# Role adapter with layer norm on one core: the b_up add on VectorE, role rows broadcast by DMA per batch, four raw slots for x and W_down

## The chip, the cores and the metric

The kernel runs on one core of one Trainium2 chip. Times are device microseconds (us) of one execution; the comparison figure is the median of several executions. Inside a core TensorE (PE) multiplies matrices, VectorE (DVE), ScalarE (ACT) and GpSimd (POOL) work on vectors, and SyncE (SP) here only issues DMAs. Each engine runs its own instruction list in order and waits on semaphores.

## The reference

Eight batches of 512 tokens of width 1024. Each batch b has a role r in {1, 2}, known only at run time, which picks one of three weight sets.

```python
# x: (8, 512, 1024); role: (8,)
h = einsum('bsh,bhk->bsk', x, W_down[role]) + b_down[role]     # 1024 -> 512
h = gelu(h)                                                    # exact form
u = einsum('bsk,bkh->bsh', h, W_up[role]) + b_up[role]         # 512 -> 1024
y = x + u
yn = (y - mean(y)) * rsqrt(var(y) + 1e-5)                      # over the 1024
return yn * gamma[role] + beta[role]
```

## The kernel before, in words

**The product.** Each float32 operand is split in two parts of the reduced float32 format that TensorE takes: `hi` is the rounded value (a cast by ScalarE), `lo` is the remainder (a subtraction by VectorE). A product is the sum of three passes, hi x hi, hi x lo, lo x hi. A batch has 96 "down" matmuls (x transposed and W_down, result `down_ps`, the hidden width in four groups `kc` of 128) and 96 "up" matmuls (h and W_up, result `up_ps`, four token tiles `t` of 128 tokens x 1024, two at a time in `up_ps`). The host gives x in both layouts, `xT` for the product and `x` for the residual sum.

**Staging.** x and W_down come in `NLOAD` = 4 parts of 512 KB each, W_up in 4 parts, the residual rows in 4 tiles, all 512 KB. The raw parts of x and W_down share `NSTAGE` = 2 slots each, so the load of part i waits for the split of part i - 2 (`x_split`, `wd_split`). W_up has one slot per part.

**The order within a batch** is written out by hand for each engine. TensorE (L284 to L332): down parts 0 and 1 over all four `kc`; then for each `kc` parts 2 and 3, so that the four groups end one after the other (`down_ready`); then up tile by tile, where tile 0 waits for `wu_split` and `h_split` of each `kc`, and each tile waits until the half of `up_ps` that it overwrites has been summed (`summed`). ScalarE (L395 to L421): casts of W_up, then for each `kc` gelu and the cast of h, between them the casts of the next batch's x and W_down parts, then for each tile the mean and the squares in two halves of 512. VectorE (L546 to L570): `wu_lo` (L551), then `h_lo` (L555) for each `kc` with `x_lo` (L480) and `wd_lo` (L485) of the next batch between them, then for each tile the sum with the row total (L497), the centring with gamma (L515) and the finish with rstd and beta (L526). The first two tiles have a next-batch split ahead of the sum. `h_full` is used again for the centred tiles, so gelu waits for `normed` of the batch before.

**GpSimd** (L444 to L461) adds b_up of the batch's role to the four tiles of residual rows (L449, `biased`, on which the sum waits), then computes rstd of each tile in three operations of 128x1. At the start it spreads b_up, gamma and beta of all three roles over the partitions (L468) from rows that SP loads into `rows`; every engine then picks the role's slice through a register. SP may not load `rows` of batch 0 before that (`params_spread`).

**SyncE** (L201 to L234) issues every DMA, in one queue: next batch's parts 0 and 1 of x and W_down, rows 0 and 1, next part 2, rows 2, next part 3, rows 3, next W_up, then the four stores as the tiles are finished. `load_rows` of a tile waits until the tile's last store has landed (`stored`).

The loop over batches 1 to 6 is a hardware loop; batch 0 and batch 7 are unrolled. In the last batch the last tile is summed in two halves.

Of the kernel before, what the change touches and what calls it, by code (L numbers as in the profile page):

```python
# [5 lines left out]
P = 128  # L23
LN_EPS = 1e-05

ALU = mybir.AluOpType
# [7 lines left out]
def bass_role_adapter_layernorm(  # L34
# [14 lines left out]
    HC = H // P  # L49
# [6 lines left out]
    NSTAGE = 2  # L56
    WARM_UP = 12
    assert KC == NLOAD and S == BANK and K == BANK and HALVES == 2 and NT == 4

    with ExitStack() as ctx:  # L60
# [17 lines left out]

# [6 lines left out]
        b_up_all = sb("b_up_all", [P, R * H], F32)  # L85
        gamma_all = sb("gamma_all", [P, R * H], F32)
        beta_all = sb("beta_all", [P, R * H], F32)
# [9 lines left out]
        var = sb("var", [P, NT, HALVES], F32)  # L97
        var_eps = sb("var_eps", [P, NT, 2], F32)
# [5 lines left out]

# [3 lines left out]

        roles_landed = sem("roles_landed")
        b_down_landed = sem("b_down_landed")  # L110
        params_landed = sem("params_landed")
        x_landed = [sem(f"x_landed{i}") for i in range(NSTAGE)]
        wd_landed = [sem(f"wd_landed{i}") for i in range(NSTAGE)]
        first_chunk_landed = sem("first_chunk_landed")
# [7 lines left out]
        first_chunk_hi = sem("first_chunk_hi")  # L122
# [20 lines left out]
        var_ready = sem("var_ready")  # L143
        half_var_eps_ready = sem("half_var_eps_ready")
        params_spread = sem("params_spread")
# [7 lines left out]
        def landed(batch, i):  # L153

            return 16 * ((NLOAD // NSTAGE) * batch + i // NSTAGE + 1)
# [5 lines left out]
        params = [(rows[32 * i:32 * i + 1, :, :].rearrange("p t h -> p (t h)")[:, 0:R * H], all_roles, param)  # L161
                  for i, (all_roles, param) in enumerate(((b_up_all, b_up), (gamma_all, gamma), (beta_all, beta)))]

        centred = h_full[:, :, :].rearrange("p (t i) s -> p t (i s)", t=2)

# [9 lines left out]

        @block.sync
        def _(sp):
            def load_x_part(batch, i):
                sp.dma_start(x_stage[:, i % NSTAGE, :],
                             xT[batch].rearrange("(p n c) s -> p n (c s)", n=NLOAD, c=CPL)[:, i, :]  # L180
                             ).then_inc(x_landed[i % NSTAGE], 16)

            def load_wd_part(role, i):
                sp.dma_start(wd_stage[:, i % NSTAGE, :],
                             W_down[role].rearrange("(p n c) k -> p n (c k)", n=NLOAD, c=CPL)[:, i, :]
                             ).then_inc(wd_landed[i % NSTAGE], 16)

            def load_first_wd_part(role):

                src = W_down[role].rearrange("(p c) k -> p (c k)", c=HC)  # L190
                sp.dma_start(wd_stage[:, 0, 0:K], src[:, 0:K]).then_inc(first_chunk_landed, 16)
                sp.dma_start(wd_stage[:, 0, K:CPL * K], src[:, K:CPL * K]).then_inc(wd_landed[0], 16)

            def load_wu_part(role, i):
                sp.dma_start(wu_stage[:, i, :],
                             W_up[role, i * P:(i + 1) * P, :]).then_inc(wu_landed[i], 16)

            def load_rows(batch, t):
                sp.dma_start(rows[:, t, :], x[batch, t * P:(t + 1) * P, :]).then_inc(rows_landed[t], 16)

            def steps(b):  # L201
                first, last = is_first(b), is_last(b)
                if not last:
                    next_role = load_role(sp, b + 1)
                    for i in range(NSTAGE):
                        sp.wait_ge(x_split, NLOAD * b + NLOAD - NSTAGE + i + 1)
                        load_x_part(b + 1, i)
                        sp.wait_ge(wd_split, NLOAD * b + NLOAD - NSTAGE + i + 1)
                        load_wd_part(next_role, i)
                if first:  # L210
                    sp.wait_ge(params_spread, len(params))
                for t in range(NT):
                    if not first:
                        sp.wait_ge(stored[t], 16 * b)
                    load_rows(b, t)
                    if not last and t in (1, 2):
                        i = NLOAD // 2 + t - 1
                        sp.wait_ge(x_split, NLOAD * (b + 1) + i - NSTAGE + 1)
                        load_x_part(b + 1, i)
                        sp.wait_ge(wd_split, NLOAD * (b + 1) + i - NSTAGE + 1)  # L220
                        load_wd_part(next_role, i)
# [4 lines left out]
                for t in range(NT):  # L226
                    if is_last(b) and t == NT - 1:
                        for i in range(HALVES):
                            sp.wait_ge(normed, NT * B + i)
# [27 lines left out]
            for t in range(NT - 1):  # L257
                sp.wait_ge(stored[t], 16 * B)
# [354 lines left out]
```

## Time and profile before

| what | value |
|---|---|
| three executions | 407.95, 413.99, 415.98 us; median 413.99 |
| the profiled execution's span | 407.0 us (the lowest of the three times is 0.95 above it) |
| busy: PE / DVE / ACT / POOL | 369.9 / 312.0 / 193.2 / 163.5 us |
| matmuls | 1548, 12 of them a warm-up |
| DMA | 84.05 MB, mean 206 GB/s |
| mean granted TensorE clock | 0.954 |

The profile gives one execution. A busy time is the union of an engine's instructions; matmuls overlap in the pipeline, so their step (start to start) says more than their duration. The granted clock is a share of full speed, 2.4 GHz; 0.5 is 1.2 GHz.

### The profile page before, as it was taken

To read this page: it belongs to the slowest core of one execution; us is meant where nothing else is said; L and a number is where in the kernel's file an instruction comes from. 1 tells how busy PE (TensorE), PEld (TensorE's weight loads), DVE (VectorE), ACT (ScalarE), POOL (GpSimd) and SP (SyncE) were. 2 spreads that over 40 slices of the span, in tenths; PEclk is the share of its full clock that TensorE was granted. 3 is DMA by queue.
4 is the path that set the end of the run, shared out by engine and by line. 5 is a ranking of instruction groups with operands and counts; after the bars stand their busy time and mean duration, and the time that the engine had idled before them with its cause. 6 is when DMAs were issued, how large, how long until landed. Compare 5 with 4: busy or idle time off the path is not lost.

```text
span 407.0 us, 5068 instructions
## 1 busy us (share of the span) xinstructions
PE 369.9 (91%) x1548; PEld 298.2 (73%) x1548; DVE 312.0 (77%) x262; ACT 193.2 (47%) x358; POOL 163.5 (40%) x138
## 2 busy tenths in 40 slices
PE   6969879988999799997999979997999959999992
PEld 2748668866888678886888868886788848888881
DVE  1899298889776996959877897769969695694475
ACT  3459434584353733565343942637335652353332
POOL 0830195247330863217621473307532164328221
PEclk8799989998999989998999989999899988999998
DMA  6489902698128862399326991287813985244022
GB/s 196 169 306 376 387 16 105 201 394 331 56 103 304 324 248 99 131 330 335 136 103 203 324 392 61 103 294 279 303 75 135 333 263 225 94 157 163 0 103 104
DMA packets 23489, 84.05 MB, mean 206 GB/s; under 512 B 2741, under 2 KB 2741, under 8 KB 23477
## 3 DMA queue, kind: packets, MB, share of 16 engines
q1 hardware_dynamic: 23480, 83.94, 56.4%
q8 instruction: 4, 0.07, 0.1%
q14 instruction: 5, 0.04, 0.0%
HBM read 67.15 MB, written 16.78 MB: 206 GB/s over the span
## 4 chain that ended last, share of the span: by engine, by line
PE 54%; DVE 16%; issue 8%; ACT 8%; DMA 7%; POOL 4%; SPq 1%; ACTq 0%; DVEq 0%; POOLq 0%
PE up_ps L279 32%; PE down_ps L271 22%; DVE wd_lo L485 4%; DVE h_lo L555 4%; DVE x_lo L480 4%; ACT x_hi L349 3%; ACT h_full L408 2%; POOL rows L449 2%; DMA x_stage<-xT 2%; DMA rows<-x 2%; DMA wu_stage<-W_up 2%; DVE rows L497 2%; DMA wd_stage<-W_down 1%; ACT squares L368 1%; DVE rows L526 1%
## 5 line engine op out<-in xcount | busy, mean ns | idle before, releaser
L449 POOL TENSOR_TENSOR rows<-rows,b_up_all 128x1024 f32<-128x1024 f32 x32 | 89.8, 2823 | 135.0 <-DMA rows<-x 109.5
L279 PE MATMUL up_ps<-wu_hi,h_hi 128*128 128x512 f32 x256 | 85.6, 415 | 20.8 <-DVE h_lo L555 16.8
L271 PE MATMUL down_ps<-x_hi,wd_hi 128*128 128x512 f32 x256 | 83.4, 397 | 7.3 <-DVE wd_lo L485 3.5
L279 PE MATMUL up_ps<-wu_lo,h_hi 128*128 128x512 f32 x256 | 83.2, 405 | 0.0
L279 PE MATMUL up_ps<-wu_hi,h_lo 128*128 128x512 f32 x256 | 83.0, 404 | 0.0
L271 PE MATMUL down_ps<-x_lo,wd_hi 128*128 128x512 f32 x256 | 82.3, 393 | 0.0
L271 PE MATMUL down_ps<-x_hi,wd_lo 128*128 128x512 f32 x256 | 81.4, 389 | 0.0
L279 PEld LDWEIGHTS up_ps<-wu_hi,h_hi 128*128 128x128 f32 x256 | 50.2, 200 | 35.2 <-issue 20.9
L480 DVE TENSOR_TENSOR x_lo<-x_stage,x_hi 128x1024 fp32r<-128x1024 f32 x32 | 60.2, 1882 | 9.5 <-ACT x_hi L349 9.5
L497 DVE SCALAR_TENSOR_TENSOR rows<-up_ps,rows 128x1024 f32<-128x1024 f32 x31 | 37.9, 1222 | 37.4 <-PE up_ps L279 29.7
L271 PEld LDWEIGHTS down_ps<-x_hi,wd_hi 128*128 128x128 f32 x256 | 48.6, 191 | 19.2 <-issue 6.8
L555 DVE TENSOR_TENSOR h_lo<-h_full,h_hi 128x512 fp32r<-128x512 f32 x32 | 42.3, 1336 | 26.2 <-ACT h_hi L411 26.1
L485 DVE TENSOR_TENSOR wd_lo<-wd_stage,wd_hi 128x1024 fp32r<-128x1024 f32 x32 | 57.3, 1791 | 4.8 <-ACT wd_hi L431 3.6
L279 PEld LDWEIGHTS up_ps<-wu_lo,h_hi 128*128 128x128 f32 x256 | 50.9, 199 | 11.2
L279 PEld LDWEIGHTS up_ps<-wu_hi,h_lo 128*128 128x128 f32 x256 | 50.3, 197 | 11.0
L375 ACT ACTIVATE neg_mean_scaled<-row_sum 128x1 f32<-128x1 f32 x31 | 6.3, 203 | 106.7 <-DVE rows L497 106.7
L271 PEld LDWEIGHTS down_ps<-x_lo,wd_hi 128*128 128x128 f32 x256 | 48.8, 191 | 10.3
L271 PEld LDWEIGHTS down_ps<-x_hi,wd_lo 128*128 128x128 f32 x256 | 48.0, 188 | 10.0
L526 DVE SCALAR_TENSOR_TENSOR rows<-h_full,rstd,beta_all 128x1024 f32<-128x1024 f32 (+1 forms) x33 | 41.2, 1252 | 11.7 <-POOL rstd L460 7.9
L408 ACT ACTIVATE h_full<-down_ps,b_down_all 128x512 f32<-128x512 f32 x32 | 21.9, 684 | 52.2 <-PE down_ps L271 52.2
L368 ACT ACTIVATE squares<-rows,neg_mean_scaled 128x512 bf16<-128x512 f32 x64 | 45.7, 715 | 0.0
L453 POOL TENSOR_TENSOR var_eps<-var,eps 128x1 f32<-128x1 f32 x32 | 14.0, 436 | 77.6 <-ACT squares L368 77.5
(36 smaller groups left out, 288.4 us busy)
## 6 DMA issues: line engine op xcount, KB each, us to landing
x_stage<-xT SPq DMA_DIRECT2D x32, 512.0 KB, 5.8
wu_stage<-W_up SPq DMA_DIRECT2D x32, 512.0 KB, 8.3
rows<-x SPq DMA_DIRECT2D x32, 512.0 KB, 7.7
wd_stage<-W_down SPq DMA_DIRECT2D x31, 512.0 KB, 6.0
out<-rows SPq DMA_DIRECT2D x31, 512.0 KB, 2.6
wd_stage<-W_down SPq DMA_DIRECT2D x2, 256.0 KB, 5.5
out<-rows SPq DMA_DIRECT2D x2, 256.0 KB, 2.0
roles_sb<-roles SPq DMA_DIRECT2D x1, 0.0 KB
```

Source lines behind the costliest of these rows:

```text
L271: return pe.matmul(down_ps[:, kc, :], wd_part[:, n, c * K + kc * P:c * K + (kc + 1) * P], x_part[:, n, c * S:(c + 1) * S], start=start, st ...
L279: mm = pe.matmul(up_ps[:, t % 2, half], h_part[:, kc, t * P:(t + 1) * P], wu_part[:, kc, half], start=(kc == 0 and h_part is h_hi and wu_p ...
L349: act.copy(x_hi[:, i, :], x_stage[:, i % NSTAGE, :]).then_inc(x_hi_ready, 1)
L368: act.activation(squares[:, half], rows[:, t, half], ACT.Square, bias=neg_mean_scaled[:, t:t + 1], scale=H ** -0.5, accum_out=var[:, t, i: ...
L408: act.activation(h_full[:, kc, :], down_ps[:, kc, :], ACT.Gelu, bias=bias).then_inc(h_full_ready, 1)
L449: pool.tensor_tensor(rows[:, t, :], rows[:, t, :], b_up_all[:, bass.ds(role * H, H)], ALU.add).then_inc(biased, 1)
L453: pool.tensor_tensor(var_eps[:, t, 0:1], var[:, t, 0:1], eps[:, :], ALU.add).then_inc(half_var_eps_ready, 1)
L480: dve.tensor_tensor(x_lo[:, i, :], x_stage[:, i % NSTAGE, :], x_hi[:, i, :].bitcast(F32), ALU.subtract).then_inc(x_split, 1)
L485: dve.tensor_tensor(wd_lo[:, i, :], wd_stage[:, i % NSTAGE, :], wd_hi[:, i, :].bitcast(F32), ALU.subtract).then_inc(wd_split, 1)
L497: dve.scalar_tensor_tensor(out=rows[:, t, :], in0=up_ps[:, t % 2, :], scalar=1.0, in1=rows[:, t, :], op0=ALU.mult, op1=ALU.add, accum_out= ...
L526: dve.scalar_tensor_tensor(out=rows[:, t, half], in0=centred[:, t % 2, half], scalar=rstd[:, t:t + 1], in1=beta_all[:, bass.ds(role * H + ...
L555: dve.tensor_tensor(h_lo[:, kc, :], h_full[:, kc, :], h_hi[:, kc, :].bitcast(F32), ALU.subtract).then_inc(h_split, 1)
```

## The change

- GpSimd no longer adds b_up. VectorE does, `bias_tile`, four adds of 128x1024 per batch: after `wu_lo` and before `h_lo` (in batch 0 after the last `h_lo`). Only rstd stays on GpSimd, two operations per tile in place of three.
- b_up, gamma and beta are no longer spread by GpSimd for all roles at the start. SP loads the role's row once per batch by a DMA that repeats it over 128 partitions (`load_role_row`), three per batch, 512 KB written each. VectorE waits for each of them at the batch's first tile.
- x and W_down have four raw slots each, so parts 0 to 3 of batch 0 are issued without a wait, and a part of the next batch waits for the split of the same part.
- SP's order is new: next part 0, rows 0, rows 1, the store of the batch before's tile 3, rows 2, gamma, beta, rows 3, next parts 1 to 3, next W_up, the next b_up (after the four adds), stores 0 to 2.
- VectorE and ScalarE put tile 3 of a batch at the start of the next one. VectorE: sum, centre, finish of that tile, `wu_lo`, adds, `h_lo` 0, next part 0, `h_lo` 1 to 3, then the sums with the next parts 1 to 3 between them. ScalarE casts the next part 0 after gelu 0, parts 1 and 2 after gelu 3, part 3 after tile 0's squares.
- Squares are one instruction of 1024 per tile but for the very last tile. TensorE's up tiles 0 and 1 wait for tiles 2 and 3 of the batch before, each for its own.
- At the start the first x part comes in two halves as the first W_down part does, and ScalarE's queue, not SP's, loads the roles and b_down.

```diff
-        x_stage = sb("x_stage", [P, NSTAGE, CPL * S], F32)
-        wd_stage = sb("wd_stage", [P, NSTAGE, CPL * K], F32)
+        x_stage = sb("x_stage", [P, NLOAD, CPL * S], F32)
+        wd_stage = sb("wd_stage", [P, NLOAD, CPL * K], F32)
...
# SyncE
+            def load_next_part(b, next_role, i):
+                sp.wait_ge(x_split, NLOAD * b + i + 1)
+                load_x_part(b + 1, i)
+                sp.wait_ge(wd_split, NLOAD * b + i + 1)
+                load_wd_part(next_role, i)
+            def load_role_row(row, param, role, landed):
+                sp.dma_start(row[:, :], param[bass.ds(role, 1), :].partition_broadcast(P)).then_inc(landed, 16)
...
             def steps(b):
+                role = load_role(sp, b)
                 if not last:
                     next_role = load_role(sp, b + 1)
+                    load_next_part(b, next_role, 0)
                 if first:
+                    load_role_row(b_up_row, b_up, role, b_up_landed)
+                load_rows(b, 0)
+                load_rows(b, 1)
+                if not first:
+                    store(b - 1, NT - 1)
+                load_rows(b, 2)
+                load_role_row(gamma_row, gamma, role, gamma_landed)
+                load_role_row(beta_row, beta, role, beta_landed)
+                load_rows(b, 3)
                 if not last:
+                    for i in range(1, NLOAD):
+                        load_next_part(b, next_role, i)
                     for i in range(KC):
                         sp.wait_ge(wu_split, KC * b + i + 1)
                         load_wu_part(next_role, i)
+                    sp.wait_ge(biased, NT * (b + 1))
+                    load_role_row(b_up_row, b_up, next_role, b_up_landed)
+                for t in range(NT - 1):
+                    store(b, t)
...
# TensorE
-                            pe.wait_ge(summed, NT * b)
+                            pe.wait_ge(summed, NT * b - 2 + t + 1)
...
# VectorE
+            def bias_tile(b, t):
+                if t == 0:
+                    dve.wait_ge(b_up_landed, 16 * (b + 1))
+                dve.wait_ge(rows_landed[t], 16 * (b + 1))
+                dve.tensor_tensor(rows[:, t, :], rows[:, t, :], b_up_row[:, :], ALU.add).then_inc(biased, 1)
+            def first_half_steps(b):
+                first, last = is_first(b), is_last(b)
+                if not first:
+                    sum_tile(b - 1, NT - 1)
+                    centre_tile(b - 1, NT - 1)
+                    finish_tile(b - 1, NT - 1)
+                split_wu(b)
+                if not first:
+                    for t in range(NT):
+                        bias_tile(b, t)
+                split_h(b, 0)
+                if not last:
+                    split_x_part(b + 1, 0)
+                    split_wd_part(b + 1, 0)
+                for kc in range(1, KC):
+                    split_h(b, kc)
+                if first:
+                    for t in range(NT):
+                        bias_tile(b, t)
+            def steps(b):
+                first_half_steps(b)
+                split_x_part(b + 1, 1)
+                split_wd_part(b + 1, 1)
+                split_x_part(b + 1, 2)
+                sum_tile(b, 0)
+                centre_tile(b, 0)
+                split_wd_part(b + 1, 2)
+                finish_tile(b, 0)
+                sum_tile(b, 1)
+                split_x_part(b + 1, 3)
+                centre_tile(b, 1)
+                split_wd_part(b + 1, 3)
+                finish_tile(b, 1)
+                sum_tile(b, 2)
+                centre_tile(b, 2)
+                finish_tile(b, 2)
...
# GpSimd
-                    pool.tensor_tensor(rows[:, t, :], rows[:, t, :], b_up_all[:, bass.ds(role * H, H)],
-                                       ALU.add).then_inc(biased, 1)
+            def inverse_deviation(b, t):
+                pool.wait_ge(var_ready, NT * b + t + 1)
+                pool.tensor_tensor(var_eps[:, t:t + 1], var[:, t:t + 1], eps[:, :], ALU.add).then_inc(var_eps_ready, 1)
+                pool.wait_ge(var_eps_ready, NT * b + t + 1)
+                pool.tensor_tensor(rstd[:, t:t + 1], var_eps[:, t:t + 1], minus_half[:, :],
+                                   ALU.pow).then_inc(rstd_ready, 1)
```

## Rows read from the trace of the kernel before

**Rows 1.** The page's first lines: span; busy us, share of the span, instructions.

```profile
span 407.0 us, 5068 instructions
PE 369.9 (91%) x1548; PEld 298.2 (73%) x1548; DVE 312.0 (77%) x262; ACT 193.2 (47%) x358; POOL 163.5 (40%) x138
```

**Rows 2.** TensorE's timeline, edges of stages: start, duration, instruction, count, idle before.

```profile
7.67 1.73 PE L271 MATMUL down_ps<-x_hi,wd_hi 128*128 128x512 f32 x4 [2.03 <-ACT wd_hi L429]
...
26.02 0.47 PE L271 MATMUL down_ps<-x_hi,wd_hi 128*128 128x512 f32 x1 [2.87 <-DVE wd_lo L485]
...
37.93 0.62 PE L279 MATMUL up_ps<-wu_hi,h_hi 128*128 128x512 f32 x2
...
52.99 1.22 PE L279 MATMUL up_ps<-wu_hi,h_hi 128*128 128x512 f32 x2 [4.01 <-DVE rows L497]
...
65.31 1.98 PE L271 MATMUL down_ps<-x_hi,wd_hi 128*128 128x512 f32 x8
...
355.52 1.98 PE L271 MATMUL down_ps<-x_hi,wd_hi 128*128 128x512 f32 x8
...
398.82 0.39 PE L279 MATMUL up_ps<-wu_hi,h_lo 128*128 128x512 f32 x1
```

**Rows 3.** Waits of TensorE: total us, times, longest.

```profile
PE up_ps L279 <- DVE h_lo L555: 16.8, 7, 4.2
PE up_ps L279 <- DVE rows L497: 4.0, 1, 4.0
PE down_ps L271 <- DVE wd_lo L485: 3.5, 2, 2.9
```

**Rows 4.** Windows around TensorE's wait before 93.53: length, busy, granted clock, DMA.

```profile
90.00:93.53 3.53, 0.00 (x0) 0.03 (x1) 3.53 (x3) 1.46 (x3) 3.53 (x2) 0.98 0.95 344
93.53:97.06 3.53, 3.53 (x8) 2.50 (x9) 3.53 (x2) 1.29 (x2) 2.08 (x1) 0.54 0.87 323
97.06:100.60 3.54, 3.54 (x17) 2.92 (x16) 3.54 (x5) 1.79 (x6) 2.32 (x1) 1.00 1.02 415
```

**Rows 5.** Groups by line and form: busy us, mean ns, idle before and releaser.

```profile
L449 POOL TENSOR_TENSOR rows<-rows,b_up_all 128x1024 f32<-128x1024 f32 x32 | 89.8, 2823 | 135.0 <-DMA rows<-x 109.5 <-issue 25.5
...
L480 DVE TENSOR_TENSOR x_lo<-x_stage,x_hi 128x1024 fp32r<-128x1024 f32 x32 | 60.2, 1882 | 9.5 <-ACT x_hi L349 9.5
...
L555 DVE TENSOR_TENSOR h_lo<-h_full,h_hi 128x512 fp32r<-128x512 f32 x32 | 42.3, 1336 | 26.2 <-ACT h_hi L411 26.1
...
L551 DVE TENSOR_TENSOR wu_lo<-wu_stage,wu_hi 128x1024 fp32r<-128x1024 f32 x32 | 37.0, 1219 | 0.1
```

**Rows 6.** Timeline of GpSimd and VectorE, three stretches: start, duration, instruction, count.

```profile
49.34 11.32 POOL L449 TENSOR_TENSOR rows<-rows,b_up_all 128x1024 f32<-128x1024 f32 x4 [25.54 <-issue]
...
58.32 1.21 DVE L497 SCALAR_TENSOR_TENSOR rows<-up_ps,rows 128x1024 f32<-128x1024 f32 x1
...
90.56 5.60 DVE L555 TENSOR_TENSOR h_lo<-h_full,h_hi 128x512 fp32r<-128x512 f32 x2
...
129.60 0.69 DVE L555 TENSOR_TENSOR h_lo<-h_full,h_hi 128x512 fp32r<-128x512 f32 x1 [3.64 <-ACT h_hi L411]
```

**Rows 7.** VectorE's timeline in the last batch: sum and finish of one tile.

```profile
383.00 1.23 DVE L497 SCALAR_TENSOR_TENSOR rows<-up_ps,rows 128x1024 f32<-128x1024 f32 x1 [3.35 <-PE up_ps L279]
...
387.18 1.29 DVE L526 SCALAR_TENSOR_TENSOR rows<-h_full,rstd,beta_all 128x1024 f32<-128x1024 f32 x1 [1.12 <-POOL rstd L460]
```

**Rows 8.** ScalarE's timeline: first gelu of a batch, and what follows its cast.

```profile
128.23 0.69 ACT L408 ACTIVATE h_full<-down_ps,b_down_all 128x512 f32<-128x512 f32 x1 [6.81 <-PE down_ps L271]
...
129.47 1.05 ACT L349 CAST x_hi<-x_stage 128x1024 fp32r<-128x1024 f32 x1
```

**Rows 9.** Windows at the start; the last three: clock, DMA share, GB/s.

```profile
0.00:10.00 10.00, 6.16 (x16) 2.40 (x16) 1.52 (x3) 3.17 (x5) 0.33 (x7) 0.90 0.66 194
...
30.00:50.00 20.00, 18.97 (x84) 15.38 (x82) 12.53 (x13) 14.12 (x18) 0.66 (x1) 1.00 1.01 384
```

**Rows 10.** The page's DMA issues: KB each, median us from issue to landing.

```profile
rows<-x SPq DMA_DIRECT2D x32, 512.0 KB, 7.7
...
out<-rows SPq DMA_DIRECT2D x31, 512.0 KB, 2.6
```

More of the change, by code:

```diff
@@ L194, in load_wu_part @@
-            def load_wu_part(role, i):
[L195 to L199, printed above, removed]
+                sp.dma_start(wd_stage[:, i, :], wd_src(role)[:, i, :]).then_inc(wd_landed[i], 16)
+            def load_next_part(b, next_role, i):
[3 more added lines that the diff above has]
+                load_wd_part(next_role, i)
@@ L201, in steps, with store @@
+            def store(b, t):
+                sp.wait_ge(normed, NT * b + t + 1)
+                sp.dma_start(out[b, t * P:(t + 1) * P, :], rows[:, t, :]).then_inc(stored[t], 16)
             def steps(b):
                 first, last = is_first(b), is_last(b)
+                role = load_role(sp, b)
                 if not last:
                     next_role = load_role(sp, b + 1)
[L205 to L209, printed above, removed]
@@ L210, in steps @@
-                if first:
[L211 to L221, printed above, removed]
+                    load_next_part(b, next_role, 0)
@@ L256, in _ @@
             steps(B - 1)
+            for i in range(HALVES):
+                sp.wait_ge(normed, NT * B + i)
+                half = slice(i * BANK, (i + 1) * BANK)
+                sp.dma_start(out[B - 1, (NT - 1) * P:NT * P, half], rows[:, NT - 1, half]).then_inc(last_stored, 16)
             for t in range(NT - 1):
@@ L392, in last_variance @@
                 act.wait_ge(scaled_mean_ready, NT * B)
-                square_halves(t)
+                for i in range(HALVES):
+                    half = slice(i * BANK, (i + 1) * BANK)
+                    act.activation(squares[:, half], rows[:, t, half], ACT.Square, bias=neg_mean_scaled[:, t:t + 1],
+                                   scale=H ** -0.5, accum_out=half_var[:, i:i + 1]).then_inc(half_var_ready, 1)
             def steps(b):
@@ L414, in steps @@
-                if not last:
-                    for i in range(NLOAD // 2, NLOAD):
-                        round_next_part(b, i)
-                for t in range(NT):
-                    if last and t == NT - 1:
-                        last_variance()
-                    else:
-                        variance(b, t)
+                round_wu(b)
+                gelu(b, 0, role)
+                if not last:
+                    round_next_part(b, 0)
+                gelu(b, 1, role)
+                gelu(b, 2, role)
@@ L424, in _ @@
+                gelu(b, 3, role)
+                if not last:
+                    round_next_part(b, 1)
+                    round_next_part(b, 2)
+                variance(b, 0)
+                if not last:
+                    round_next_part(b, 3)
+                variance(b, 1)
+                variance(b, 2)
+            act.dma_start(roles_sb[:, :], roles).then_inc(roles_landed, 16)
+            act.dma_start(b_down_all[:, :], b_down_cols).then_inc(b_down_landed, 16)
             act.wait_ge(constants_ready, 2)
@@ L526, in finish_tile @@
                     dve.scalar_tensor_tensor(out=rows[:, t, half], in0=centred[:, t % 2, half],
[L527 to L528 removed]
+                                             scalar=rstd[:, t:t + 1], in1=beta_row[:, half],
                                              op0=ALU.mult, op1=ALU.add).then_inc(normed, 1)
[L531 removed]
+            def first_half_steps(b):
[9 more added lines that the diff above has]
+                split_h(b, 0)
+                if not last:
+                    split_x_part(b + 1, 0)
[3 more added lines that the diff above has]
+                if first:
+                    for t in range(NT):
+                        bias_tile(b, t)
```

275 lines of the change are left out of this document (119 added, 156 removed).

## The prediction

> **What bounds the kernel now.** I read the page's busy shares, the waits of TensorE, its timeline at the edges of the batches, and the clock around one of its waits. The span is 407.0 us and PE is busy 91% of it [rows 1]. All 1536 matmuls of the product (1548 less 12 of the warm-up) are the same size and run back to back at one step: from the last batch's first down matmul to its last up matmul, 355.52 to 398.82, lie 191 steps, 0.2267 us each [rows 2], so a batch of 192 costs 43.5 us, and eight cost 348.2 us. That leaves 58.8 us: 7.7 before the first matmul, 7.9 after the last one (398.82 + 0.23 to 407.0), and 43.2 lost between. The reader should see in [rows 2] that batch 0 takes 57.6 us (7.67 to 65.31: 14.1 lost) and batches 1 to 6 take 290.2 (65.31 to 355.52: 29.1 lost, 4.85 each). Batch 7 loses nothing.
>
> The waits name the losers [rows 3]: 16.8 us for h_lo (7 times), 4.0 once for the summed rows, 3.5 for wd_lo. Each long h_lo wait is followed by a second loss: in the 3.5 us after the wait that ends at 93.53 the granted clock is 0.54, and it was 0.98 and 1.00 before and after; only 8 matmuls begin in it, 17 in the next 3.5 us [rows 4]. By the half steps that is some 1.7 us a time: 16.8 + 6 x 1.7 = 27 of the 29.1.
>
> Why is h_lo late? VectorE. A subtraction 128x1024 takes 1.22 us where GpSimd is idle (wu_lo) and 1.88 on average as x_lo; the h_lo of half that size takes 0.69 alone and 5.60 for two while GpSimd adds b_up [rows 5, 6]. A sum whose first input lies in PSUM takes 1.21 us in the middle of GpSimd's add [rows 6]: only instructions with two SBUF inputs are held. The Trainium skill (SBUF — State Buffer, Who interferes with whom) has a rule of that shape: such an instruction shares a read port with GpSimd under an exclusive lock. By that, the trace agrees.
>
> **Part 1, the add moves.** Removed: 32 GpSimd adds, 89.8 us [rows 5], and the stretch of VectorE beside them: x_lo 32 x (1.88 - 1.22) = 21, h_lo 32 x (1.34 - 0.69) = 21, and wd_lo, of x_lo's shape and count, taken as a little less than it: some 60 us. Added to VectorE: 32 adds with two SBUF inputs; not in the trace, the nearest row is wu_lo, the same shape, 1.22, or 1.15 start to start: 37 to 39 us, and never less than nothing. Net some 20 us of VectorE, but what matters is where it lies. GpSimd keeps two 128x1 operations per tile.
>
> I lay out a steady batch from its first down matmul (0), which is how the order in the diff has it:
> - VectorE: sum, centre and finish of the previous tile 3. In the last batch of the trace this very order takes 383.00 to 388.47, 5.5 us [rows 7], so it ends at 5.6. Four wu_lo: 10.2. Four adds, if their rows have landed: 14.8.
> - ScalarE: the first gelu can start at 13.75, 0.15 after the third quarter's first group; gelu and cast take 1.24 (128.23 to 129.47) [rows 8]. So h_hi 0 is there at 15.0, x and W_down part 0 of the next batch at 16.9, h_hi 1 at 18.2, h_hi 2 at 20.4, h_hi 3 at 23.2.
> - TensorE wants h_lo 0 at 21.8, 1 at 23.1, 2 at 24.5, 3 at 25.8.
> - VectorE from its last add: h_lo 0, x_lo, wd_lo, h_lo 1 are 0.65 + 1.15 + 1.15 + 0.65 = 3.6 us. From 14.8 that gives 18.4 or, held by h_hi 1, 18.9: 4 us early. Later: sum 0 ends at 28.7 where TensorE wants it at 32.6; sum 1 at 34.0, wanted at 38.1; wd_lo 3 at 37.5, wanted at 54.4. VectorE's work is 36 us in 43.5.
> So the h_lo wait goes, and with it the low clock: 29.1 us. What is late next is tile 3's rows.
>
> **Part 2, queues and waits.** Three added DMAs per batch (b_up, gamma, beta to 128 partitions), 512 KB written each, go on SP's queue; the trace has no such transfer. In the stretch 30 to 50 the queue moved 384 GB/s, so a transfer of 512 KB costs 1.37 us [rows 9]. A batch had 20 of them, now 23: 31.5 us in 43.5, hidden. But the order matters: store of tile 3, rows 2, gamma, beta, rows 3, and rows 3 waits until that store has landed. VectorE's fourth add waits for rows 3, and behind it stand h_lo 0 to 3. SP starts at 0.7; x 0, W_down 0, rows 0, rows 1, store, rows 2, gamma, beta, rows 3 are nine transfers, the first 2.6 us like a lone store [rows 10]: 0.7 + 2.6 + 8 x 1.37 = 14.3. The other bound: issued at 9.9 plus the median 7.7 of rows [rows 10] is 17.6. TensorE isn't hit until 18.3 (18.3 + 1.2 + 3.6 = 23.1). I take no wait; slack is 0.7 to 4 us. A broadcast could also be cheaper than a load, since it reads one row; below 1.37 it changes nothing here, as it is hidden.
>
> The Trainium skill (DMA: Bandwidth & Descriptors, Rules for kernel authors) speaks against broadcasts whose outermost dimension is small: a leading repeat of c copies keeps the whole transfer on at most c engines. Here the repeat is 128, by which all 16 would work; if it were lowered as one row repeated inside, the rule would give the far end of rival (b). No row shows which.
>
> **Part 3, the start.** Removed: three 12 KB loads, three GpSimd broadcasts (4 us each) and the wait of x and W_down parts 2, 3 for a free slot. TensorE waited 2.87 us until 26.02 and again 0.7 for wd_lo [rows 2, 3]. With four slots the eight parts and W_up are issued by 9 us. TensorE was through with the first two parts at 23.0 (26.02 less 2.87 and the 0.16 by which an end trails the next start). The eight parts are 4.2 MB: 1.9 MB had moved by 10 us, the rest at 384 GB/s is there at 15.9 [rows 9], and ScalarE and VectorE add 3.6: 19.5, so nothing waits. Down of batch 0 then ends at 23.0 + 48 x 0.2267 = 33.9, not 37.93 [rows 2]: 4.0 saved. Bounds: the split first x chunk may bring 1 us more; a slower landing behind more queued transfers may take 3 back. The two small loads on ScalarE's queue cost it 1 us before anything has landed: nothing.
>
> **Part 4, batch 0's second half.** TensorE waited 4.0 us until 52.99 [rows 2, 3] for sum 0, which waited for GpSimd's adds, which waited for the parameter setup, then ran slow for 1.7. Now: h_lo 3 at 35.9 (33.9 + 0.15 + 1.24 + 0.65), four adds 40.5 (rows 3 is the 21st transfer, 11 MB, by the same rate at 34), x_lo 1, wd_lo 1, x_lo 2 at 44.0, sum 0 at 45.2. TensorE wants it at 44.8: 0.4 left of 5.7, saved 5.2 (2 to 5.7). The weaker wait of up for the sums costs and brings nothing: tile 2's sum was long done. One square of 1024 in place of two of 512, one GpSimd operation less per tile: off the path. The last tile keeps its form, the tail keeps its 7.9 us.
>
> **Sum.** 407.0 - 29.1 - 4.0 - 5.2 = 368.7 us span. The lowest of the three runs lies 0.95 above the span, so the profiled execution would be 369.7. The median shown is 6.0 above that run, for no reason the trace shows; I carry half of it: 373. A measurement of this kernel tells about 2% from no change.
>
> **Rivals.**
> (a) The wait survives, smaller: rows 3 lands after 18.3, or VectorE trails. For it: the median landing of rows, 7.7, is only 0.7 from the limit, and any wait seems to cost 1.7 more in clock. A stall of 1 plus 1.7 in six batches is 16 us: 389. Against: no transfer in 30 to 50 was slow. With a stall in only some batches it is 380.
> (b) Slower: the broadcasts are slow, all reading one 4 KB row. Each us above 1.37 on gamma and beta delays rows 3 by 2. At 3.4 us each the stall begins; at 4.9 each batch loses as much as before; from 6.4 on the kernel is over 2% slower. At 7 us: rows 3 at 25.6, stall 7.3 + 1.7 = 9.0, that is 4.15 more than now in six batches, 24.9, less the 9.2 of batch 0: 407.0 + 15.7 = 423, with the same addition 427. Against: the loads in the trace have 4 KB pieces too and run at 384 GB/s; for: nothing shows a repeated source. The far end is a broadcast confined to one of sixteen engines, 16 x 1.37 = 22 us: then the queue itself binds, 20 x 1.37 + 3 x 22 = 93 us a batch, some 750 in all; 0.01 of the chance.
> (c) The change doesn't reach: VectorE becomes the bound because its adds stand in front of h_lo and GpSimd's small operations still hold it. It would need 8 us more VectorE work per batch; then the h_lo loss is replaced one for one and only the start improves: 402. Against: 7.5 us of VectorE slack per batch.
>
> **Chances.** Forecast (no steady wait, 366 to 378) 0.62; (a) 0.25, of which a tenth lands within 2%; (c) 0.05; (b) 0.05, 0.04 of it slower; unforeseen 0.03. Faster by over 2%: 0.87; within 2%: 0.08; slower: 0.05. The range takes the forecast and most of (a): 366 to 390.
>
> **What would show it.** Right: no h_lo row among TensorE's waits, batches 1 to 6 at 43.5 us each, granted clock 1.00 from 16 us on; x_lo, wd_lo and h_lo at 1.22, 1.22 and 0.69 mean; adds of 1.22 on VectorE; down of batch 0 ending near 34; the tail at 7.9. Wrong: VectorE waiting for the load of rows before its fourth add and PE for h_lo behind it; gamma and beta taking over 3.4 us each; the third part of batch 0 landing after 20 us.

## The result, and the profile after

| | before | changed |
|---|---|---|
| median of the executions | 414.0 us (407.95 to 415.98) | 378.75 us (377.03 to 379.82) |
| ratio, 95% interval | | 0.9275 [0.9195, 0.9356] |
| span of the profiled execution | 407.0 us | 374.9 us |
| its own time | | 377.03 us |
| mean granted TensorE clock | 0.954 | 0.994 |

Faster by 7.2%, inside the range, 5.8 us above the forecast of 373. The page's first lines of the changed kernel, as in [rows 1]:

```profile
span 374.9 us, 4895 instructions
...
PE 355.9 (95%) x1548; PEld 289.0 (77%) x1548; DVE 288.3 (77%) x293; ACT 184.0 (49%) x297; POOL 41.1 (11%) x71
```

VectorE has 31 instructions more and is busy 24 us less. The groups by line and form show why; the rows of before are [rows 5]:

```profile
L479 DVE TENSOR_TENSOR rows<-rows,b_up_row 128x1024 f32<-128x1024 f32 x32 | 38.7, 1224 | 30.8 <-DMA rows<-x 30.7
...
L456 DVE TENSOR_TENSOR x_lo<-x_stage,x_hi 128x1024 fp32r<-128x1024 f32 x32 | 39.0, 1219 | 7.3 <-ACT x_hi L405 3.9 <-ACT x_hi L321 3.3
...
L472 DVE TENSOR_TENSOR h_lo<-h_full,h_hi 128x512 fp32r<-128x512 f32 x32 | 20.9, 685 | 5.7 <-ACT h_hi L348 5.7
```

The add costs 1.22 us, x_lo fell from 1.88 to 1.22, h_lo from 1.34 to 0.69: all as forecast. The new thing stands at the end of the first row: VectorE stood idle 30.7 us before its adds, waiting for loads of rows. TensorE's waits, against [rows 3]:

```profile
PE up_ps L251 <- DVE h_lo L472: 7.2, 7, 2.2
...
PE up_ps L251 <- DVE rows L484: 1.8, 2, 1.6
```

and its timeline at the edges and after each wait, against [rows 2]:

```profile
6.84 2.41 PE L244 MATMUL down_ps<-x_hi,wd_hi 128*128 128x512 f32 x8 [0.94 <-ACT wd_hi L407]
...
29.06 0.61 PE L251 MATMUL up_ps<-wu_hi,h_hi 128*128 128x512 f32 x2
...
41.74 0.73 PE L251 MATMUL up_ps<-wu_hi,h_hi 128*128 128x512 f32 x2 [1.63 <-DVE rows L484]
...
77.41 0.70 PE L251 MATMUL up_ps<-wu_hi,h_hi 128*128 128x512 f32 x2 [2.23 <-DVE h_lo L472]
80.28 0.70 PE L251 MATMUL up_ps<-wu_hi,h_hi 128*128 128x512 f32 x2 [1.25 <-DVE h_lo L472]
...
124.87 0.70 PE L251 MATMUL up_ps<-wu_hi,h_hi 128*128 128x512 f32 x2 [0.78 <-DVE h_lo L472]
169.29 0.70 PE L251 MATMUL up_ps<-wu_hi,h_hi 128*128 128x512 f32 x2 [0.65 <-DVE h_lo L472]
...
366.72 0.39 PE L251 MATMUL up_ps<-wu_hi,h_lo 128*128 128x512 f32 x1
```

Four numbers take a span apart and are used for every kernel below: the start of the first up matmul; the 1439 steps from there to the last matmul, 326.2 us at 0.2267; what that stretch takes above 326.2, the excess; and the tail behind the last matmul. The four add up to the span, within 0.25 for the last step. The excess is more than the waits that the profile lists: nine of them here, 9.0 us in all, go with 11.4 of excess, some 0.27 more for each.

| span | kernel | first up matmul | excess | tail |
|---|---|---|---|---|
| 407.0 | before | 37.9 | 34.7 | 8.0 |
| 368.7 | forecast | 33.9 | 0.4 | 7.9 |
| 374.9 | changed | 29.1 | 11.4 | 8.0 |

So the start gave 8.9 us where 4.0 were forecast, and the h_lo wait did not go. That is rival (a): 9.0 of the 11.4 us of excess lie in batches 1 to 6, behind h_lo, and 2.4 in batch 0, behind the sums.

**Where the wait comes from.** Batch 2 starts at 100.80. SyncE's timeline and VectorE's, of the changed kernel:

The loads and stores, on SyncE:

```profile
102.10 0.33 SPq L185 DMA_DIRECT2D out<-rows  x1
104.73 0.36 SPq L161 DMA_DIRECT2D x_stage<-xT  x1
105.28 0.35 SPq L164 DMA_DIRECT2D wd_stage<-W_down  x1
105.88 0.85 SPq L178 DMA_DIRECT2D rows<-x  x2
107.17 0.35 SPq L185 DMA_DIRECT2D out<-rows  x1
...
108.74 0.39 SPq L181 DMA_DIRECT2D beta_row<-beta  x1
115.09 0.33 SPq L178 DMA_DIRECT2D rows<-x  x1
```

and the adds, on VectorE:

```profile
112.43 1.23 DVE L479 TENSOR_TENSOR rows<-rows,b_up_row 128x1024 f32<-128x1024 f32 x1 [0.89 <-DMA rows<-x]
...
116.20 1.22 DVE L479 TENSOR_TENSOR rows<-rows,b_up_row 128x1024 f32<-128x1024 f32 x1 [1.13 <-DMA rows<-x]
120.02 1.23 DVE L479 TENSOR_TENSOR rows<-rows,b_up_row 128x1024 f32<-128x1024 f32 x1 [2.59 <-DMA rows<-x]
121.16 0.69 DVE L472 TENSOR_TENSOR h_lo<-h_full,h_hi 128x512 fp32r<-128x512 f32 x1
```

Read it as a chain. The store of tile 3 is issued at 107.17 and has landed at 115.0, 7.8 us, behind four loads; only then may rows 3 be issued, 115.09; it lands 4.9 later behind gamma and beta; the fourth add starts at 120.02, 19.2 us into the batch, past the 18.3 that the prediction named; h_lo 1 starts 4.0 later and TensorE waits 0.78. The chain closes on itself without TensorE. VectorE's waits for TensorE's tiles are three, all in the last batch:

```profile
DVE rows L484 <- PE up_ps L251: 4.1, 3, 3.4
```

From the fourth add VectorE works down its list, with short waits for ScalarE and GpSimd, to the finish of the next tile 3, on which the next store waits. Store, load of rows 3 and that list make 44.4 to 44.7 us a batch from batch 2 on, and TensorE, which needs 43.5, follows.

### The profile page after: what moved, and what is told of

Read it like the earlier page. It is cut to its first block, busy times and chain, and to the rows that moved or that the text cites. A ratio compares the mean times of both kernels' runs of the same rounds, so it can differ in the third digit from the quotient of the medians.

```text
span 374.9 us, 4895 instructions
## 1 busy us (share of the span) xinstructions
PE 355.9 (95%) x1548; PEld 289.0 (77%) x1548; DVE 288.3 (77%) x293; ACT 184.0 (49%) x297; POOL 41.1 (11%) x71
## 4 chain that ended last, share of the span: by engine, by line
DMA 25%; DVE 22%; PE 17%; issue 14%; POOL 9%; ACT 5%; SPq 5%; ACTq 1%; DVEq 1%; POOLq 0%
DMA out<-rows 12%; PE up_ps L251 11%; DVE rows L484 8%; DMA rows<-x 8%; POOL rstd L427 6%; PE down_ps L244 6%; DMA x_stage<-xT 5%; DVE x_lo L456 4%; DVE wd_lo L461 3%; DVE rows L515 3%; DVE h_lo L472 3%; ACT squares L356 3%; POOL var_eps L425 2%; ACT neg_mean_scaled L353 1%; SPq L178 1%
## 5 line engine op out<-in xcount | busy, mean ns | idle before, releaser
L251 PE MATMUL up_ps<-wu_hi,h_hi 128*128 128x512 f32 x256 | 80.3, 392 | 9.0 <-DVE h_lo L472 7.2
L251 PE MATMUL up_ps<-wu_lo,h_hi 128*128 128x512 f32 x256 | 79.6, 389 | 0.0
L251 PE MATMUL up_ps<-wu_hi,h_lo 128*128 128x512 f32 x256 | 79.5, 389 | 0.0
L479 DVE TENSOR_TENSOR rows<-rows,b_up_row 128x1024 f32<-128x1024 f32 x32 | 38.7, 1224 | 30.8 <-DMA rows<-x 30.7
L515 DVE SCALAR_TENSOR_TENSOR rows<-h_full,rstd,beta_row 128x1024 f32<-128x1024 f32 (+1 forms) x33 | 41.2, 1252 | 22.7 <-POOL rstd L427 21.4
L501 DVE SCALAR_TENSOR_TENSOR h_full<-rows,neg_mean,gamma_row 128x1024 f32<-128x1024 f32 (+1 forms) x33 | 41.2, 1251 | 10.0 <-ACT neg_mean L354 9.4
L425 POOL TENSOR_TENSOR var_eps<-var,eps 128x1 f32<-128x1 f32 x31 | 10.1, 326 | 322.9 <-ACT squares L356 322.9
L456 DVE TENSOR_TENSOR x_lo<-x_stage,x_hi 128x1024 fp32r<-128x1024 f32 x32 | 39.0, 1219 | 7.3 <-ACT x_hi L405 3.9
L461 DVE TENSOR_TENSOR wd_lo<-wd_stage,wd_hi 128x1024 fp32r<-128x1024 f32 x32 | 39.0, 1219 | 2.0 <-ACT wd_hi L409 1.8
L467 DVE TENSOR_TENSOR wu_lo<-wu_stage,wu_hi 128x1024 fp32r<-128x1024 f32 x32 | 37.3, 1219 | 0.2
```

The costliest lines, as they stand in the source:

```text
L251: mm = pe.matmul(up_ps[:, t % 2, half], h_part[:, kc, t * P:(t + 1) * P], wu_part[:, kc, half], start=(kc == 0 and h_part is h_hi and wu_p ...
L425: pool.tensor_tensor(var_eps[:, t:t + 1], var[:, t:t + 1], eps[:, :], ALU.add).then_inc(var_eps_ready, 1)
L456: dve.tensor_tensor(x_lo[:, i, :], x_stage[:, i, :], x_hi[:, i, :].bitcast(F32), ALU.subtract).then_inc(x_split, 1)
L461: dve.tensor_tensor(wd_lo[:, i, :], wd_stage[:, i, :], wd_hi[:, i, :].bitcast(F32), ALU.subtract).then_inc(wd_split, 1)
L467: dve.tensor_tensor(wu_lo[:, i, :], wu_stage[:, i, :], wu_hi[:, i, :].bitcast(F32), ALU.subtract).then_inc(wu_split, 1)
L479: dve.tensor_tensor(rows[:, t, :], rows[:, t, :], b_up_row[:, :], ALU.add).then_inc(biased, 1)
```

## The experiments

The ratios are to the kernel before, run beside each.

| kernel | median us | ratio [95%] | span | first up matmul | excess | tail |
|---|---|---|---|---|---|---|
| changed, with gamma and beta after rows 3 | 373.0 | 0.9141 [0.9056, 0.9227] | 371.5 | 29.6 | 7.5 | 8.0 |
| changed, fourth add late | 367.72 | 0.9031 [0.8951, 0.9111] | 366.0 | 30.2 | 1.4 | 8.0 |
| changed, adds on GpSimd | 381.68 | 0.9372 [0.929, 0.9454] | 379.3 | 29.2 | 15.7 | 8.0 |
| before, adds alone | 375.86 | 0.9221 [0.9139, 0.9302] | 373.9 | 38.4 | 0.0 | 9.1 |
| before, one piece of the order alone | 389.47 | 0.958 [0.9512, 0.9649] | 387.2 | 39.0 | 13.8 | 8.0 |
| three moves together | 370.11 | 0.9104 [0.9055, 0.9153] | 366.5 | 29.1 | 2.9 | 8.0 |

The eleven executions of the kernel before that stand beside the last two rows spread from 403.69 to 411.81 us, so these two ratios are less sure than their intervals. What is said of these kernels below rests in the main on waits and spans.

**1. Is it the landing of rows 3?** Two edits of the changed kernel. The loads of gamma and beta behind rows 3:

```diff
-                load_role_row(gamma_row, gamma, role, gamma_landed)
-                load_role_row(beta_row, beta, role, beta_landed)
                 load_rows(b, 3)
+                load_role_row(gamma_row, gamma, role, gamma_landed)
+                load_role_row(beta_row, beta, role, beta_landed)
```

> The changed kernel with the loads of gamma and beta issued after rows 3 instead of before. Theory: the rest of the h_lo wait comes from the landing of rows 3 (store of tile 3 landed, then rows 3 takes 4.9 us behind gamma and beta, at 19.2 us of the batch). It should then land in about 2.6 to 3 us, some 2 us earlier, and TensorE's waits for h_lo (7.2 us in 7 times) fall to nearly nothing except in batch 1: span 374.9 - 5 = about 370. Rival, VectorE itself trails (its last tiles end 1 us late and its in-order list is the limit): span stays at 375 and the wait for rows turns into another wait of VectorE.

Measured: the h_lo wait fell from 7.2 us to 3.1 and the excess from 11.4 to 7.5. In batch 2 rows 3 still waits for the store to land, and lands 3.3 us after its issue instead of 4.9. First VectorE's timeline, then SyncE's with the issue of rows 3:

```profile
107.81 4.62 DVE L467 TENSOR_TENSOR wu_lo<-wu_stage,wu_hi 128x1024 fp32r<-128x1024 f32 x4
...
119.35 1.23 DVE L479 TENSOR_TENSOR rows<-rows,b_up_row 128x1024 f32<-128x1024 f32 x1 [1.02 <-DMA rows<-x]
```

```profile
116.05 0.33 SPq L178 DMA_DIRECT2D rows<-x  x1
116.56 0.33 SPq L181 DMA_DIRECT2D gamma_row<-gamma  x1
```

So 1.6 of the 2 us are there, and 3.4 of the 5 us of span; the store's landing, the longer half of the chain, stays. The gain does not show in the landing counted from batch 2's first matmul, 19.1 us, since VectorE trails TensorE further here; it shows in the length of the batches, 43.5 to 44.0 us from batch 3 on. By the ratios alone this kernel can't be told from the changed one (the intervals meet); the waits tell them apart.

The fourth add behind the last h_lo:

```diff
                 if not first:
-                    for t in range(NT):
+                    for t in range(NT - 1):
                         bias_tile(b, t)
                 split_h(b, 0)
...
-                if first:
-                    for t in range(NT):
-                        bias_tile(b, t)
+                for t in range(NT) if first else [NT - 1]:
+                    bias_tile(b, t)
```

> The changed kernel with the fourth add (tile 3) moved behind the last h_lo in batches 1 to 7. Theory: h_lo no longer stands behind the landing of rows 3; rows 2 lands at 15.4 us of the batch, so h_lo 1 is ready at about 20.5 where TensorE wants it at 23.1: no h_lo wait from batch 2 on, span 369 to 371. Rival (VectorE's amount of work): the add is paid for later, sum 0 comes later than TensorE wants tile 2, and the span stays at 375.

Measured: no h_lo wait at all; span 366.0, below what was expected, ratio clear of the changed kernel's. TensorE's waits in full, the warm-up's own left out:

```profile
PE down_ps L244 <- ACT wd_hi L409: 1.2, 1, 1.2
...
PE down_ps L244 <- ACT wd_hi L407: 1.1, 1, 1.1
PE up_ps L251 <- DVE rows L484: 0.6, 2, 0.5
```

The rival is out: the same work of VectorE, one add 5 us later (24.0 us into batch 2, not 19.2), and 10 of the 11 us of excess are gone. The wait was a load in front of h_lo in an in-order list.

**2. Is it the move of the adds that cured h_lo?** The adds go back to GpSimd, everything else changed:

```diff
 # GpSimd, per batch ahead of the rstd steps
+                for t in range(NT):
+                    if t == 0:
+                        pool.wait_ge(b_up_landed, 16 * (b + 1))
+                    pool.wait_ge(rows_landed[t], 16 * (b + 1))
+                    pool.tensor_tensor(rows[:, t, :], rows[:, t, :], b_up_row[:, :], ALU.add).then_inc(biased, 1)
 # VectorE: bias_tile and its calls removed
```

> The changed kernel, all of it, but the four adds of b_up go back to GpSimd (same orders, broadcasts, slots). Theory (the adds on GpSimd hold VectorE's instructions with two SBUF inputs): mean h_lo goes back above 1.1 us and x_lo or wd_lo above 1.4, the h_lo wait is 2 to 3 us in each of six batches with up to 1.7 us of low clock behind each: span 390 to 397. Rival (the new orders and slots bring the gain, not the move of the adds): span 370 to 377, since GpSimd's adds run beside VectorE and free 4.6 us of its list.

Measured: 379.3 us of span, between the two. The instructions are held again, as the theory said:

```profile
L466 DVE TENSOR_TENSOR x_lo<-x_stage,x_hi 128x1024 fp32r<-128x1024 f32 x32 | 53.7, 1678 | 8.8 <-ACT x_hi L321 4.6 <-ACT x_hi L405 4.1
...
L482 DVE TENSOR_TENSOR h_lo<-h_full,h_hi 128x512 fp32r<-128x512 f32 x32 | 32.6, 1050 | 28.6 <-ACT h_hi L348 28.6
```

but from batch 2 on TensorE waits only 0.8 to 1.3 us a batch, where before it was 2.1 to 4.2 and mostly with the low clock behind it. So the theory's size fell: the rest of the change cures most of it with the adds still on GpSimd. Beside that rest, as it stands, the move of the adds brings only 4.4 us of span (379.3 to 374.9), and the two ratios' intervals meet.

The other side, the kernel before with nothing but the adds moved, each just ahead of its sum:

```diff
                         split_next_part(b, NLOAD // 2 + t)
+                    bias_tile(b, t, role)   # waits rows_landed, adds b_up_all of the role
                     sum_tile(b, t)
```

> The kernel before with one part alone: the adds of b_up on VectorE, each just ahead of its tile's sum; two slots, the parameter broadcasts by GpSimd at the start and the orders as before. Theory: h_lo, x_lo and wd_lo at their short durations (0.69, 1.22, 1.22), no h_lo wait, 43.5 to 44.5 us a batch from batch 1 on: the 29 us of batches 1 to 6 come from this part alone, the 13 us of batch 0 do not: span 378 to 384. Rival (the orders matter as much): span above 390, with VectorE late for TensorE's tiles.

Measured: excess 0.0. From the first up matmul to the last TensorE never waits; 373.9 us span, less than expected because batch 0's wait for the sum went too, and 1.1 us longer in the tail, since VectorE comes to the last tiles late. This one edit reaches the time of the whole change: 0.9221 against 0.9275, intervals on top of each other. What the rest of the change wins at the start, 9 us, it gives back in the excess, 11 us.

And one piece of the order alone, on the kernel before, adds on GpSimd (the next batch's part 1 behind the last gelu and the last h_lo):

```diff
-                    if not last and kc < NLOAD // 2:
-                        split_next_part(b, kc)
+                    if not last and kc == 0:
+                        split_next_part(b, 0)
+                if not last:
+                    split_next_part(b, 1)
 # the same two lines in ScalarE's list, round_next_part
```

> The kernel before with one piece of the new order alone: ScalarE's casts and VectorE's splits of the next batch's part 1 come after the last gelu and the last h_lo, not between h_lo 1 and 2. The adds stay on GpSimd, two slots. Theory after the runs so far (either fewer instructions in front of h_lo 2 and 3, or short ones, is enough, so the two parts of the change don't add up): the h_lo wait falls below 1 us a batch and the low clock behind it goes, span 380 to 390. Rival (only the move of the adds cures it): span 400 to 407.

Measured: no h_lo wait; the excess falls from 34.7 to 13.8. But the wait has a new place, the sum of tile 0 (11.6 us in seven waits), now that two held splits more stand ahead of it:

```profile
PE up_ps L279 <- DVE rows L497: 11.6, 7, 2.3
PE down_ps L271 <- DVE wd_lo L485: 4.3, 3, 3.2
```

The adds hold VectorE as before; the order changes what they hold. In batch 2 three h_lo have started before GpSimd's first add, and the splits of part 1 run beside it, at nearly three times their price:

```profile
128.95 0.69 DVE L555 TENSOR_TENSOR h_lo<-h_full,h_hi 128x512 fp32r<-128x512 f32 x1 [1.40 <-ACT h_hi L411]
129.41 8.65 POOL L449 TENSOR_TENSOR rows<-rows,b_up_all 128x1024 f32<-128x1024 f32 x3 [13.70 <-DMA rows<-x]
132.62 3.18 DVE L480 TENSOR_TENSOR x_lo<-x_stage,x_hi 128x1024 fp32r<-128x1024 f32 x1 [0.17 <-ACT x_hi L349]
```

Order and move overlap: 21 us from the one, 34.7 from the other, on a loss of 34.7.

**3. What made the start faster than forecast?** Three kernels, each the changed one with one piece undone, one execution of each; then a second execution of the last of them and of the changed kernel. The edits, shortened (the casts and waits that go with them are left out, and so is the wait of the load of rows 0 for the small loads):

```diff
 # b_down and three 12 KB loads back on SyncE's queue behind part 1
+                if i == 1:
+                    sp.dma_start(b_down_all[:, :], b_down_cols).then_inc(b_down_landed, 16)
+                    for j, param in enumerate((b_up, gamma, beta)):
+                        sp.dma_start(rows[32 * j:32 * j + 1, ...], param).then_inc(params_landed, 16)
 # the first x part whole, in one load and one cast
-            sp.dma_start(x_stage[:, 0, 0:S], ...); sp.dma_start(x_stage[:, 0, S:CPL * S], ...)
+            load_x_part(0, 0)
 # the waits of two slots
             for i in range(1, NLOAD):
+                if i >= 2:
+                    sp.wait_ge(x_split, i - 1)
                 load_x_part(0, i)
+                if i >= 2:
+                    sp.wait_ge(wd_split, i - 1)
                 load_wd_part(first_role, i)
```

> The changed kernel with b_down and three 12 KB parameter loads (unused) back on SyncE's queue behind part 1 of x and W_down. Question: why did the second half of W_down's first part land in time for a cast at 7.33 us, not 10.49 as before. If the small loads held the queue: that cast moves to 9 or later and down of batch 0 ends at 31 or later instead of 29.1. If the whole queue being filled early does it: both stay within 0.5 us.

> The changed kernel with the first x part in one load and one cast. If the split x chunk moved the start: the first matmul goes from 6.84 to about 7.5 and down of batch 0 ends 0.5 to 1 us later. If not: within 0.2 us.

> The changed kernel with the start's parts 2 and 3 waiting for the split of parts 0 and 1, as two slots would make them. If the slots are what removed the waits in down of batch 0: parts 3 land at about 17 to 19, TensorE waits 2 to 4 us for their splits, down of batch 0 ends at 31 to 33. If the wait came from GpSimd's broadcasts that held VectorE (x_lo and wd_lo 3.7 to 4.2 us): at most 1 us.

> The same as the run with the waits of two slots at the start, a second look. Open: the cast of W_down's second half began at 9.28, 9.77 and 10.49 in the three kernels that issue parts 2 and 3 late, and at 7.2 to 8.5 in the five that issue all parts at once. If the early issue does it, here again 9 or later; if it is scatter from run to run, anything from 7 to 10.5.

> The changed kernel, a second look, beside the run before it: that cast at 7.2 to 8.5 if the early issue does it; waits for h_lo again 0.6 to 1.0 us in batches 2 to 6.

| kernel | span | first matmul | cast of W_down's second half | first up matmul |
|---|---|---|---|---|
| changed | 374.9 | 6.84 | 7.33 | 29.1 |
| changed, again | 378.3 | 6.78 | 8.76 | 30.5 |
| small loads back | 377.4 | 6.87 | 7.21 | 29.3 |
| first x part whole | 376.7 | 8.16 | 8.10 | 30.1 |
| two-slot waits | 379.7 | 7.53 | 9.28 | 32.9 |
| two-slot waits, again | 383.0 | 6.97 | 7.72 | 31.9 |

The small loads cost nothing. The split x chunk brings 1.3 us at the first matmul; 1.0 by the first up matmul, less than the 1.4 between the two executions of the changed kernel. The two-slot waits cost 1.4 to 3.8 us, and in both executions TensorE waits for wd_lo of part 3, 1.6 and 2.2 us. When the second half of W_down lands scatters from run to run: the repeated kernels gave 8.76 and 7.72 where 7.33 and 9.28 had been, so the early issue of the other parts does not decide it alone. That it plays no part is not shown: the kernels with the late issue lie at 7.72 to 10.49, the others at 7.21 to 8.76.

What is left, from 31.9 or 32.9 up to the 37.9 of before, has two parts. The larger lies ahead of part 2: TensorE is through with parts 0 and 1 at 23.0 before, at 18.6 and 20.1 with the two-slot waits, at 18.2 in the changed kernel. It waits for no split there. Before, it starts 0.8 us later than changed, waits 1.76 for the cast of W_down's second half, and works at the low clock: twelve matmuls from 11.16 to 15.73 us, 4.6 us where 2.7 would do. The window of before, with the granted clock third from the end, 0.60 (half speed up to about 15 us; in the changed kernel the clock is 1.00 throughout):

```profile
11.16:15.73 4.57, 4.57 (x13) 3.62 (x13) 4.09 (x2) 3.15 (x3) 3.70 (x2) 0.60 0.51 176
```

The clock falls there at 8 us, before the first broadcast (12.03), so that is not the cause; why only the kernels with the old start show it stays open. The smaller part are the waits for wd_lo of parts 2 and 3. Behind 23.0 before loses 4.1 us, the two-slot kernel 1.9 and 2.5 in its two executions. The 1.6 to 2.2 between are what the GpSimd broadcasts can have cost. In the timeline of before, VectorE at the start had

```profile
12.87 3.68 DVE L480 TENSOR_TENSOR x_lo<-x_stage,x_hi 128x1024 fp32r<-128x1024 f32 x1 [0.43 <-ACT x_hi L349]
...
16.46 4.18 DVE L485 TENSOR_TENSOR wd_lo<-wd_stage,wd_hi 128x1024 fp32r<-128x1024 f32 x1
...
20.56 4.18 DVE L480 TENSOR_TENSOR x_lo<-x_stage,x_hi 128x1024 fp32r<-128x1024 f32 x1
```

three splits at three times their price beside PARTITION_BROADCAST, 12.0 us where 3 x 1.22 would do: 8.4 lost on VectorE. The first two were done before TensorE wanted them; behind the third stood the wd_lo of part 2, for which TensorE waited 2.87 us. That these make up the 1.6 to 2.2 is argued, not shown: no kernel had the broadcasts alone put back.

**4. The three moves together.** Fourth add late, gamma and beta after rows 3, and batch 0's first sum ahead of the next batch's splits:

```diff
                 first_half_steps(b)
+                if is_first(b):
+                    sum_tile(b, 0)
                 split_x_part(b + 1, 1)
                 split_wd_part(b + 1, 1)
                 split_x_part(b + 1, 2)
+                if not is_first(b):
                     sum_tile(b, 0)
```

> The changed kernel with three moves: fourth add behind the last h_lo, gamma and beta loaded after rows 3, and in batch 0 the sum of tile 0 ahead of the next batch's splits. Theory: no wait of TensorE after batch 0's first part is left; 8 x 43.52 + 7.9 + about 7 to 9 at the start = 363.5 to 365.5 us span, against 366.0 with the add alone moved. If VectorE's order has another wait hidden behind these, 366 or more.

Measured: 366.5 us span, 370.11 median. That is the second branch of what was expected. It beats the changed kernel and not the one with the fourth add alone moved (0.9104 against 0.9031, intervals that meet). Waits of 0.1 to 0.4 us stayed, for h_lo and for sums. The lowest median here is that of the kernel with the single late add.

## Why the prediction was right, and where it was not

**The bound.** Right. TensorE's step is 0.2267 in every kernel and the tail 8.0 in all but one; 43.5 us a batch was reached for the whole of the up and down work in the kernel with the adds alone.

**Part 1, the price of the move.** Right in each duration: 1.22 for the add, 1.22 and 0.69 for the splits. Right too that VectorE's slack would hold the adds. The 29.1 us credited to it came in full in the kernel with the adds alone. What it missed is that the move is not the only cure of h_lo: one piece of the new order, on its own, removes the h_lo wait with the splits still held, though it leaves 13.8 us of excess elsewhere. The prediction treated the order as the frame in which the move was costed and never priced it by itself.

**Part 2, the queue.** This is the term that failed: rows 3 at 14.3 to 17.6 us into the batch and so "no wait". It landed at 19.2. Two of its numbers were mis-sized. SyncE was to start the batch's loads at 0.7; the store of tile 2 waits for VectorE, which trails TensorE by 1.3 us there, and 2.6 us of register work and loop lie between that store and the first load, so it is 3.9. And five transfers, up to the landing of the store, took 10.2 us, not 2.6 + 4 x 1.37 = 8.1, though the queue moves 411 GB/s in the stretch 15 to 35 of the changed kernel, more than in [rows 9]; the first, a load, took 4.1 by itself, where the sum had the 2.6 of a lone store. The upper bound fell for the same reason: it had rows 3 issued at 9.9, and the store kept it back until 14.3. The order of the loads and the threshold, 18.3, were right, and so was the rule that any later landing comes back as a wait for h_lo. The first sign that the prediction named for being wrong, VectorE waiting for rows before its fourth add and TensorE for h_lo behind it, is what the trace shows.

**Rival (a)** is what happened, but its price was 16 us for six batches, and 9.0 came. The stalls were 0.65 to 0.9 in batches 2 to 6 and 3.5 in batch 1, and the 1.7 us of low clock behind each did not come; see below.

**Rival (b)**, slow broadcasts, is out: the stretch 15 to 35 holds b_up, gamma and beta of batch 0 at 411 GB/s; gamma and beta land 1.3 us behind the transfer ahead of each, b_up 2.2. By the rule of the Trainium skill on small leading repeats (DMA: Bandwidth & Descriptors, Rules for kernel authors), a repeat of 128 may use all 16 engines; the trace agrees, with the DMA share at 1.03 in that stretch:

```profile
15.00:35.00 20.00, 20.00 (x90) 16.56 (x89) 17.45 (x18) 13.43 (x17) 0.00 (x0) 1.00 1.03 411
```

**Rival (c)**, VectorE's work as the bound, is out: with the fourth add late the same work leaves 1.4 us of excess.

**Part 3, the start**: 4.0 forecast, 8.9 measured. Down of batch 0 was to end at 33.9 because the first two parts were carried over unchanged up to 23.0. In the changed kernel TensorE is through with them at 18.2. It began 0.8 earlier, had no wait of 1.8 in the middle, and the slow matmuls around that wait (twelve from 11.16 to 15.73 behind it, in the timeline of before) did not come. The 4.0 itself, for the waits behind 23.0, was right: 4.1 came. The 4.8 ahead of it the prediction had at nothing, but for a bound of 1 us for the split first chunk, and part of it is scatter, since the second execution of the changed kernel was through with the two parts at 19.6.

**Part 4, batch 0's second half**: 0.4 of wait forecast, 1.6 and 0.2 measured. The mechanism, three splits and four adds ahead of the first sum, is the one forecast; TensorE came there 4.8 us earlier, while the next batch's loads did not. One reading of the prediction does not hold: the adds of before did not wait for the parameter setup. The last broadcast ended at 23.8 and the rows of tile 0 had landed at 38.1, but the first add began at 49.34; for these 11 us the profile names no cause.

**The sum.** 368.7 + 11.0 (waits) - 4.8 (start) = 374.9. Two errors of opposite sign; the total was near by that luck, not because each term was. From the span to the median 4.3 us were forecast, 0.95 and 3.3, and 3.9 came, but split otherwise: the profiled execution took 377.03, 2.1 above its span, the median 1.7 more.

## What to carry to other kernels

Where an in-order engine mixes work that waits for memory with work that another engine is waiting for, the first kind belongs behind the second: one add moved behind four short subtractions was worth more here than shortening the load that it waited for. A change of several parts should be costed part by part against the same loss, since two cures of one stall don't add up; here one of them alone gave the time of all. And a store that must land before a reload is two queue passages, not one.

## What the runs showed of the hardware, unexpected

**The clock.** In the kernel before, a wait of 2.22 us dropped the granted clock to 0.52 for the next 3.5 us, which is mostly the 1.2 GHz level; in the changed kernel a wait of 2.23 did not, and neither did 1.25 more 1.6 us later. Windows of the kernel before around its wait (the last three numbers are granted clock, DMA share, GB/s):

```profile
138.90:141.18 2.28, 0.06 (x2) 0.03 (x1) 2.28 (x2) 1.04 (x1) 2.28 (x2) 0.99 0.92 311
141.18:144.70 3.52, 3.52 (x8) 2.49 (x9) 3.52 (x2) 2.03 (x2) 2.08 (x1) 0.52 0.95 365
```

and of the changed kernel around its two waits in batch 1:

```profile
75.17:77.41 2.24, 0.01 (x1) 0.03 (x1) 1.97 (x3) 1.30 (x2) 0.00 (x0) 1.00 1.02 249
77.41:79.03 1.62, 1.62 (x6) 1.01 (x6) 1.62 (x2) 1.05 (x1) 0.00 (x0) 1.00 0.95 364
79.03:80.28 1.25, 0.01 (x1) 0.03 (x1) 1.25 (x3) 0.48 (x1) 0.00 (x0) 1.00 1.02 419
```

In the second execution of the changed kernel the wait was 2.89 at the same place, and after 1.05 more the matmuls ran slow (two took 1.19, not 0.70). The kernel before shows both sides by itself: at the start a wait of 2.87 us, until 26.02, left the clock at 1.00. Over all the profiled executions, the first 10 us aside, a drop followed waits from 1.89 us up, and waits of up to 2.87 passed without one; none of 0.6 to 0.9 in batches 2 to 6 brought it. So the length of a wait alone does not tell its price, and what else decides it stays open; a flat 1.7 us per wait, as the prediction took, was too much.

**The start scatters.** The same program had the cast of W_down's second half at 7.33 and at 8.76 us. That alone, 1.4 us, is of the size of an effect that one would read from a single execution.
